# Causal masks added by fp32r instead of bf16 matmuls in an attention and feed-forward kernel

## What is computed

```python
q = (x @ Wq).reshape(2, 2048, 32, 32)
k, v = (x @ Wkv)[..., :32], (x @ Wkv)[..., 32:]     # one key/value head for 32 query heads
scores = einsum('bqhd,bkd->bhqk', q, k) * 32 ** -0.5
scores = where(pos_k <= pos_q, scores + slope[h] * (pos_k - pos_q), -inf)
y = layernorm(x + (softmax(scores) @ v) @ Wo)
out = layernorm(y + y @ W.T + b + lora(y))          # a low-rank term whose rank a gate picks per row
```

## Time and profile before

| | |
|---|---|
| time before, median of 3 runs | 4225.33 us (4214.77 to 4237.7) |
| span of the profiled execution, first to last instruction | 4202.6 us |
| mean granted TensorE clock | 0.949 of full speed |
| attention, from the first to the last score tile of pass S | 79.9 to 3293.3 us |
| PE busy; weight loader (PEld) busy | 92%; 56% |
| DVE, ACT, POOL busy | 59%, 46%, 32% |

### The profile page before, as it was taken

One profiled execution on the slowest core, in us unless ns is written; L12 is line 12 of the kernel. 1 busy time (PEld: TensorE's weight loads), 2 busy tenths in 40 slices (PEclk: granted clock), 3 DMA queues, 4 the chain that ended last, 5 costly groups with the idle time before them and its releaser, 6 DMA issues. The chain is left out here.

```text
span 4202.6 us, 73921 instructions
## 1 busy us (share of the span) xinstructions
PE 3850.6 (92%) x22065; PEld 2340.6 (56%) x22065; DVE 2472.1 (59%) x4462; ACT 1929.4 (46%) x3253; POOL 1359.6 (32%) x420
## 2 busy tenths in 40 slices
PE   5989989999999998789999999999999599999998
PEld 3555544444444443555554444544443388888887
DVE  4566666666766672556666656766675244444444
ACT  2445645565666565344555656566565401000000
POOL 1114434444444454112433444445454200000010
PEclk8899989999999998899998999999998799999999
DMA  2111110000000001111001000000000311111111
GB/s 72 47 51 27 28 41 22 20 21 16 19 19 14 19 6 34 54 44 49 26 26 43 19 22 22 14 19 14 19 14 6 131 56 60 60 60 60 60 60 51
DMA packets 159069, 152.11 MB, mean 36 GB/s; under 512 B 8388, under 2 KB 141508, under 8 KB 156584
## 3 DMA queue, kind: packets, MB, share of 16 engines
q1 hardware_dynamic: 158696, 147.70, 11.9%
HBM read 96.75 MB, written 33.62 MB: 31 GB/s over the span
## 5 line engine op out<-in xcount | busy, mean ns | idle before, releaser
L509 ACT ACTIVATE prob<-ps_s,alibi 128x512 f32<-128x512 f32 (+3 forms) x2560 | 1524.5, 623 | 1193.3 <-PE ps_s L774 603.4
L589 DVE TENSOR_REDUCE mxp<-ps_a 128x1 f32<-128x512 f32 (+3 forms) x2560 | 1457.6, 605 | 910.2 <-PE ps_a L707 462.5
L452 POOL TENSOR_TENSOR prob<-prob 128x2048 f32<-128x2048 f32 (+1 forms) x240 | 1043.8, 4349 | 1298.2 <-ACT prob L509 1298.2
L771 PE MATMUL ps_s<-qst,kexp 97*128 97x512 f32 (+3 forms) x2560 | 1107.2, 444 | 84.8 <-ACT prob L509 52.8
L771 PEld LDWEIGHTS ps_s<-qst,kexp 97*128 97x128 f32 x2560 | 504.1, 198 | 905.9 <-ACT prob L509 710.4
L707 PE MATMUL ps_a<-kmax,qst 97*128 97x512 f32 (+3 forms) x2560 | 950.3, 397 | 29.2 <-DMA qst<-qst 13.4
L794 PE MATMUL ps_o<-prob,val 128*32 128x512 f32 (+3 forms) x5120 | 624.8, 562 | 0.0
L707 PEld LDWEIGHTS ps_a<-kmax,qst 97*128 97x128 f32 x2560 | 503.3, 197 | 107.6 <-DVE mxp L589 52.7
L794 PE MATMUL ps_sum<-prob,ones 128*32 128x512 f32 (+3 forms) x3200 | 384.8, 569 | 0.1
L980 POOL TENSOR_TENSOR hb_sb<-h_sb,bias_b 128x1024 f32<-128x1024 f32 x32 | 76.9, 2402 | 790.9 <-DVE z_sb L1124 731.1
L607 DVE RECIPROCAL r_sb<-s_sb 128x128 f32<-128x128 f32 x256 | 233.8, 931 | 122.0 <-ACT s_sb L515 119.8
(11 more groups left out here) (148 smaller groups left out, 3672.5 us busy)
## 6 DMA issues: line engine op xcount, KB each, us to landing
wq_raw<-in_L_attn_Wq SPq DMA_DIRECT2D x65, 512.0 KB, 3.8
xs<-in_L_attn_hidden_states SPq DMA_DIRECT2D x9, 2048.0 KB, 8.1
qst<-qst SPq DMA_DIRECT2D x64, 256.0 KB
att_scratch<-at_sb SPq DMA_DIRECT2D x64, 256.0 KB, 2.3
at_raw<-att_scratch SPq DMA_DIRECT2D x32, 512.0 KB, 5.4
x_sb<-in_L_attn_hidden_states SPq DMA_DIRECT2D x32, 512.0 KB, 4.3
out<-z_sb SPq DMA_DIRECT2D x32, 512.0 KB, 3.1
z_sb<-in_L_attn_Wo SPq DMA_DIRECT2D x4, 512.0 KB, 5.3
```

Of the source, the lines that this page charges most:

```text
L452: nc.gpsimd.tensor_tensor(even[:, :, c1:], even[:, :, c1:], odd[:, :, c1:], ALU.add).then_inc(pair_done, 1)
L509: nc.scalar.activation(prob[slot][:, h, c0:], ps_s[bank][:, c0:], ACT.Exp, bias=alibi_of(u, h, k - QT * s)).then_inc(e_done, 1)
L589: nc.vector.tensor_reduce(mxp[:, h * QT + t, c:c + 1], ps_a[bank][:, 0:cols], AX.X, ALU.max).then_inc(a_done, 1)
L771: last = nc.tensor.matmul(ps_s[bank][:, c0:], kexp[0:KR, k * P:(k + 1) * P], qst[buf][0:KR, h, c0:], start=True, stop=not diagonal)
```

## The change

The bf16 identity and the two bf16 masks are replaced by fp32r ones. POOL makes fp32 masks (mask_q, mask_k) and the fp32 identity that is there anyway; DVE casts the three to fp32r, which is three more 128x128 copies at the start. The two mask matmuls read the fp32r tiles. POOL has one memset and one select less, and DVE waits for all of POOL's nine constants instead of seven of its eleven before its first cast; the semaphore counts follow.

```diff
-        identb = sb(ctx, "identb", [P, P], BF16)
-        maskb = sb(ctx, "maskb", [P, P], BF16)
-        maskt = sb(ctx, "maskt", [P, P], BF16)
+        identr = sb(ctx, "identr", [P, P], F32R)
+        mask_q = sb(ctx, "mask_q", [P, P], F32)
+        mask_k = sb(ctx, "mask_k", [P, P], F32)
+        maskr_q = sb(ctx, "maskr_q", [P, P], F32R)
+        maskr_k = sb(ctx, "maskr_k", [P, P], F32R)
...
-        VEC_C = 2 * NH + 3 + 2 * QT + 8
+        VEC_C = 2 * NH + 6 + 2 * QT + 8
...
-            sp.wait_ge(vec_c, 2 * NH + 3 + 2 * QT)
+            sp.wait_ge(vec_c, 2 * NH + 6 + 2 * QT)
...
-            nc.gpsimd.memset(identb[:], 0.0).then_inc(pool_c, 1)
-            nc.gpsimd.memset(maskb[:], 0.0).then_inc(pool_c, 1)
-            nc.gpsimd.memset(maskt[:], 0.0).then_inc(pool_c, 1)
+            nc.gpsimd.memset(mask_q[:], 0.0).then_inc(pool_c, 1)
+            nc.gpsimd.memset(mask_k[:], 0.0).then_inc(pool_c, 1)
...
-            dve.wait_ge(pool_c, 7)
+            dve.wait_ge(pool_c, 9)
             nc.vector.tensor_copy(dist[:], dist_i[:]).then_inc(vec_c, 1)
             nc.vector.tensor_copy(kmax[3 * DH:KR], kpos_i[3 * DH:KR]).then_inc(vec_c, 1)
-            dve.wait_ge(vec_c, NH + 3)
+            nc.vector.tensor_copy(identr[:], ident[:]).then_inc(vec_c, 1)
+            nc.vector.tensor_copy(maskr_q[:], mask_q[:]).then_inc(vec_c, 1)
+            nc.vector.tensor_copy(maskr_k[:], mask_k[:]).then_inc(vec_c, 1)
+            dve.wait_ge(vec_c, NH + 6)
...
-                    last = nc.tensor.matmul(ps[:, cols - P:cols], identb[:], maskb[:], start=False, stop=True)
+                    last = nc.tensor.matmul(ps[:, cols - P:cols], identr[:], maskr_q[:], start=False, stop=True)
...
-                            last = nc.tensor.matmul(ps_s[bank][:, c0:c0 + P], identb[:], maskt[:], start=False,
+                            last = nc.tensor.matmul(ps_s[bank][:, c0:c0 + P], identr[:], maskr_k[:], start=False,
                                                     stop=True)
```

More of the change, by code:

```diff
@@ L11 @@
 F32R = mybir.dt.float32r
-BF16 = mybir.dt.bfloat16
 I32 = mybir.dt.int32
@@ L414, in _ @@
             nc.gpsimd.memset(ident[:], 0.0).then_inc(pool_c, 1)
-            nc.gpsimd.memset(identb[:], 0.0).then_inc(pool_c, 1)
-            nc.gpsimd.memset(maskb[:], 0.0).then_inc(pool_c, 1)
-            nc.gpsimd.memset(maskt[:], 0.0).then_inc(pool_c, 1)
+            nc.gpsimd.memset(mask_q[:], 0.0).then_inc(pool_c, 1)
+            nc.gpsimd.memset(mask_k[:], 0.0).then_inc(pool_c, 1)
             nc.gpsimd.memset(ones[:], 1.0).then_inc(pool_c, 1)
             nc.gpsimd.iota(dist_i[:], [[P, DIST0 + QT]], base=-P * DIST0, channel_multiplier=1).then_inc(pool_c, 1)
+            pool.wait_ge(pool_c, 5)
+            nc.gpsimd.iota(kpos_i[3 * DH:KR], [[1, T]], base=0, channel_multiplier=0).then_inc(pool_c, 1)
             pool.wait_ge(pool_c, 6)
[L421 to L426, removed]
+            nc.gpsimd.affine_select(out=ident[:], in_=ident[:], compare_op=ALU.not_equal, fill=1.0, base=0,
                                     pattern=[[-1, P]], channel_multiplier=1).then_inc(pool_c, 1)
-            nc.gpsimd.affine_select(out=maskt[:], in_=maskt[:], compare_op=ALU.is_ge, fill=MASKED, base=0,
+            nc.gpsimd.affine_select(out=mask_q[:], in_=mask_q[:], compare_op=ALU.is_ge, fill=MASKED, base=0,
+                                    pattern=[[-1, P]], channel_multiplier=1).then_inc(pool_c, 1)
+            nc.gpsimd.affine_select(out=mask_k[:], in_=mask_k[:], compare_op=ALU.is_ge, fill=MASKED, base=0,
                                     pattern=[[1, P]], channel_multiplier=-1).then_inc(pool_c, 1)
@@ L545, in _ @@
             nc.vector.tensor_copy(wkvh[:, :, 3 * DH:P], wkv_raw[:, :, DH:2 * DH]).then_inc(vec_c, 1)
-            dve.wait_ge(vec_c, 2 * NH + 3 + 2 * QT + 4)
+            dve.wait_ge(vec_c, 2 * NH + 6 + 2 * QT + 4)
             for r in range(3):
@@ L648, in _ @@
         def _(pe):
-            pe.wait_ge(pool_c, 11)
+            pe.wait_ge(pool_c, 9)
             pe.wait_ge(vec_c, NH)
```

## The result

| | before | changed |
|---|---|---|
| median, 20 runs each | 4215.47 us (4194.82 to 4237.7) | 4233.44 us (4213.9 to 4253.11) |
| ratio changed / before | | 1.0033, 95% interval 1.002 to 1.0047 |
| span of the profiled execution | 4202.6 us | 4243.2 us |
| its mean granted clock | 0.949 | 0.939 |
| span times clock | 3988 us | 3984 us |

The change makes the kernel slower by 0.33%, 14 us (the two medians lie 18 us apart). That is inside the 0.5% that I called no change, but the interval leaves out 1, and I had forecast 4 us less. The last two lines of the table say where to look. Span times clock is what the span would be if TensorE had run at full clock and all of the time shrank with it. It is nearly the same in the two profiled executions; they differ in how much ran at the lower of TensorE's two clocks.

A forecast was written before the change was run, and what follows sets the result against it. PE, busy 92% of the 4202.6 us span, was taken as the bound. Masks -5 us and start +1 us gave -4 us, so 4225.3 - 4 = 4221 us; the 8-in-10 range was 4186 to 4250 us.

The forecast's parts named there:

- The load is brought forward to its tile's start: At each mask matmul: the fp32r weight load starts with the matmul before it and blocks for 0.11 us.
- the 205 us rival: At all 2048 masks: the fp32r load starts only at the tile's end, 100 ns each, 205 us, 4430 us; chance 6%.
- From a short tile to its mask: Behind 128-column tiles, 512 masks: 0.11 us to the mask's start in place of 0.06, as the load is not hidden.
- The sum: All masks: 26 us gained behind 1536 wider tiles, 19.5 us lost behind 512 short ones; net 6.5 gained, 5 let through.
- The share of 8 in 10: All mask effects on PE: 8 in 10 of each reaches the end; the rest meets PE's waits for ACT or DVE.
- The 164 us: All 2048 mask loads: losing the fast weight load, 80 ns more each, taken as a price alone; paid only behind short tiles.
- The start: Kernel start: constants ready 0.3 us later and three casts of 0.7 us, +1.0 us with nothing covering it; bounds 0.5 to 1.5.
- The total work: Whole kernel: masks -5 us and the start +1 us, -4 us against the profiled span of 4202.6 us.
- The starting point: Whole kernel before: median of the runs, 22.7 us above the profiled span, 4225.3 us, from which 4 us were taken.
- The step that failed: TensorE's clock: assumed unchanged; as a rival, a 0.015 shift either way gives 4197 or 4245 us, chances 5% and 6%.
- the 46 ns: Behind each of 512 128-column tiles: loss from the fp32r load's 0.11 us in place of 0.06, by the trace's finer values.

The follow-up runs named there:

- e_wide: Changed kernel's start, fp32r masks only behind tiles of 256 columns or more, bf16 masks behind 128-column tiles; against the kernel before: ratio 1.0007.
- e_start: Kernel before with the changed kernel's start and three casts more, all masks still bf16; against the kernel before: ratio 1.0007.
- e_short: Changed kernel's start, fp32r masks only behind 128-column tiles, bf16 masks behind wider ones; against the kernel before: ratio 1.0084.
- e_nomask: Changed kernel without its 2048 mask matmuls, so causal masking is left out; against the kernel before: ratio 0.9815.
- the repeat: The changed kernel run again, unaltered, beside the kernel before on one chip: ratio 1.0042.
- e_thick: Changed kernel with its 512 tiles of 128 columns and their fp32r masks made 256 columns wide; against the kernel before: ratio 0.9973.

## Why the prediction was right or wrong

- **The load is brought forward to its tile's start.** Right; the rows show it behind 128 and 256 columns, and the 205 us rival is out. The rule in the Trainium skill that I held against it ("TensorE: Matmul & The Clock Gate", section "The mechanism", and not the section that the prediction names), that a load overlaps running matmuls only where its row group differs, is contradicted by the mask's own load as well: it starts at 65.79 with its tile, though tile (97 rows) and mask (128 rows) share rows of the array.
- **From a short tile to its mask 0.11 in place of 0.06 us, behind the mask 0.11 to 0.12 in place of 0.12.** Right.
- **The sum.** 1536 x 17 ns gained and 512 x 38 ns lost, net 5 us after waits. Measured at an equal clock: 9 us gained (e_wide less e_start) and 13 us lost (e_short less e_start), where 26 x 0.8 = 21 and 19.5 x 0.8 = 16 stood; by span times clock 12 gained and 5 lost. Either way the gain was sized too high. By the first reading the net is a loss of 4 us and not a gain, by the second a gain of 6; the runs can't settle that sign. The share of 8 in 10 that I let through is one reason: for all masks together it is 126 of 240 us, 5 in 10 (e_nomask). The 164 us that the prediction worked out from the Trainium skill ("TensorE: Matmul & The Clock Gate", section "Weight-path perf modes") take a factor of four, which the page gives as theory for fp8, while it gives about two as measured. In the traces the two loads are recorded at 0.10 and 0.19 us, and the 164 us enter no sum.
- **The start.** +1.0 us forecast. The first transpose starts at 21.82 in place of 21.02, +0.8 us. The run with the start alone measured 3.7 us with an error of 3, too coarse for it.
- **The total work.** -4 us forecast; span times clock moved by -4 us in the profiled pair and by -4 us in the repeat, and by the equal-clock reading +2.2, good to 3. Right that the work hardly changes.
- **The starting point.** The 4221 us were taken from the median of three runs, 4225.3. Over 20 runs the kernel before has 4215.5. So 4221 lies 12 us below the 4233 measured, but the change itself was missed by 18 us or more (-4 forecast; +14 by the ratio, +18 by the medians). That the forecast time comes as near is in part luck.
- **The step that failed** is the clock: "I see no reason for a shift in the change, since PE does nearly the same work in nearly the same time." The mean clock fell by 0.0051 and that is 16 of 18.6 us. I had even read the price off, 16 us for 0.01 (the runs give 32), and then held the clock fixed, taking the sum of the work for what the clock depends on. The runs show that it isn't: filling matmuls with no use raise it to 0.9665, wider short tiles to 0.9574, and the variants differ in the time at the lower clock at the unit ends (257 us before, 320 changed). There, behind the 1.7 us wait for the shifts, at 1.2 GHz, the short tiles of pass S run, and with fp32r masks the clock came back later. An fp32r mask there takes 0.11 us in place of 0.06 for the same columns at the higher clock. The reason may have stood in my own sum, as the 46 ns; e_thick speaks for it but does not prove it.
- The masks behind wide tiles lower the clock too, by 0.0026, without taking any streaming away, and the account above has no reason for that. Without any masks it falls to 0.9326, though that saves time.
- What stays open: the fall behind the wide tiles; that the clock's fall in the two parts adds up to 0.0086 against 0.0051 for the whole, more than the errors of 0.001 allow; where pass A's short tiles lose it; and whether the type has an effect of its own, which no run here separates from the load.

## What to carry to other kernels

Where TensorE is the bound and its mean granted clock is below 1, compare mean clock and span times clock before span: an edit that leaves the work alone can still move the time through the clock. Look at what stands behind each wait that precedes a fall; filling a wait of under 2 us, repeated in every unit, with three matmuls of no use of their own took 49 us off this kernel. And behind a matmul shorter than the weight load of its successor (here 128 columns, 0.06 us, against 0.11) the load shows: here the type with the shorter load did better there. The other type behind the wider tiles paid only once the wait was filled.

## What the runs showed that was not expected

- A mean clock of 0.9475 became 0.9642 to 0.9665 with matmuls in the wait, and 0.9574 with short tiles and their masks twice as wide: more work, less time.
- A bf16 load behind an fp32r matmul was not brought forward: it starts at the tile's end (66.16), while the fp32r load of the same mask in the changed kernel starts with the tile. Nothing is lost by it, as the load is short.
- Without the masks the kernel is only 1.85% faster, though their starts add up to 5.7% of the span.
